# Cross-attention of a four-block kernel: the maximum over partitions by a turned row and a product of ones, the key bias as one product, other PSUM banks for the outputs, and an order of its own for each engine

## The reference, cut to what matters

```python
n = layernorm(x)                                            # per token, over 128 features
Sim = (n @ w1)[:, :, None] + (ctx @ w2)[:, None, :] + einsum('bid,bjd->bij', n * w3, ctx) + b_sim
A = softmax(Sim, axis=2)                                    # over the 77 context rows
hat = A @ ctx
Batt = softmax(max(Sim, axis=2), axis=1)                    # over the 512 tokens
hc = einsum('bi,bid->bd', Batt, n)                          # one vector for a batch element
feats = concat([n, hat, n * hat, n * hc[:, None, :]])
x = x + feats @ W_qv + b_qv
```

## Time and profile before

| | us |
|---|---|
| median of three runs | 1986.94 |
| the profiled execution | 1985.58 |
| its span in the trace | 1983.8 |
| first block, to the end of its last instruction | 108.74 |
| first instructions of the second block | 109.58 |
| mean granted TensorE clock over the span | 0.97 of full |

### The profile page before, as it was taken

The page is one execution under the profiler, slowest core; times in us unless marked ns, Lnnn a source line. Parts: engine busy times, 40 slices in busy tenths (PEclk is TensorE's granted clock), DMA queues, the critical chain, the costliest instruction groups (busy, mean ns, idle before and its releaser), DMA issues. The chain is left out here.

```text
span 1983.8 us, 78949 instructions
## 1 busy us (share of the span) xinstructions
PE 1823.7 (92%) x32837; PEld 1278.3 (64%) x32837; DVE 1430.1 (72%) x2605; ACT 1138.5 (57%) x2379; POOL 1435.6 (72%) x1838
## 2 busy tenths in 40 slices
PE   4769999999999999999999999999999999788948
PEld 3636666666666666666666666666666676566638
DVE  2268778778777788787878787877788778455546
ACT  1136666666566566666666566656666666335425
POOL 1168888879788888888888788978898888222334
PEclk9789999999999999999999999999999999889969
DMA  3022131111311113111113111121111101030012
GB/s 101 1 41 56 44 99 52 47 45 51 101 48 48 51 48 100 49 50 48 48 48 103 48 48 46 34 85 32 32 35 36 42 24 35 10 98 1 23 35 71
DMA packets 60837, 99.93 MB, mean 50 GB/s; under 512 B 15848, under 2 KB 35065, under 8 KB 58643
## 3 DMA queue, kind: packets, MB, share of 16 engines
q1 hardware_dynamic: 58978, 91.72, 16.0%
q0 software_dynamic: 1504, 3.17, 0.5%
HBM read 44.50 MB, written 21.45 MB: 33 GB/s over the span
## 5 line engine op out<-in xcount | busy, mean ns | idle before, releaser
L1273 PE MATMUL b_bank_proj<-layer_weights,b_stream_t 128*128 128x512 f32 x1152 | 591.6, 615 | 13.6 <-DVE b_plain_moved L1069 9.7
L1069 DVE TENSOR_TENSOR b_plain_moved<-b_bank_proj,b_rope 128x1024 f32<-128x1024 f32 x384 | 467.6, 1221 | 100.2 <-ACT b_squares L903 96.9
L812 POOL TENSOR_TENSOR b_rotated<-b_plain_moved 128x1024 f32<-128x1024 f32 x192 | 453.4, 2361 | 45.4 <-DVE b_plain_moved L1069 45.4
L827 POOL TENSOR_TENSOR b_rotated<-b_rotated,b_inv_norm 128x1024 f32<-128x1024 f32 x192 | 365.3, 1902 | 15.1
L903 ACT ACTIVATE b_squares<-b_bank_proj 128x512 f32<-128x512 f32 x384 | 229.2, 597 | 248.4 <-PE b_bank_proj L1273 243.4
L1273 PEld LDWEIGHTS b_bank_proj<-layer_weights,b_stream_t 128*128 128x128 f32 x1152 | 187.9, 191 | 117.1 <-issue 57.1
L1075 DVE TENSOR_REDUCE b_norm<-b_squares 128x16 f32<-128x1024 f32 x192 | 232.2, 1209 | 42.7 <-ACT b_squares L903 42.4
L1281 PEld LDWEIGHTS b_bank_shared<-const_tables,b_rotated 128*128 128x128 f32 x1536 | 180.6, 143 | 72.2 <-issue 67.4
L1281 PE MATMUL b_bank_shared<-const_tables,b_rotated 128*128 128x128 f32 x1536 | 211.9, 276 | 3.8 <-POOL b_rotated L827 1.7
L832 POOL TENSOR_TENSOR b_probs<-b_probs,b_inv_sum 128x512 f32<-128x512 f32 x192 | 200.3, 1047 | 14.0 <-DVE b_inv_sum L1090 13.8
L1347 PEld LDWEIGHTS b_bank_shared<-b_attended_t,layer_weights 128*128 128x128 f32 x1536 | 182.9, 192 | 25.6 <-issue 23.9
(11 more groups left out here) (346 smaller groups left out, 2889.7 us busy)
## 6 DMA issues: line engine op xcount, KB each, us to landing
b_v_shifted<-b_v SPq DMA_DIRECT2D x192, 192.0 KB, 2.5
sorted_rows<-sorted_rows SPq DMA_DIRECT2D x66, 258.0 KB, 3.2
layer_weights<-L_ffn_Wqkv SPq DMA_DIRECT2D x6, 1536.0 KB
b_v_shifted<-b_v SPq DMA_DIRECT2D x72, 128.0 KB
layer_weights<-L_ffn_Wo SPq DMA_DIRECT2D x6, 512.0 KB
c_sorted_in<-sorted_rows SPq DMA_DIRECT2D x23, 129.0 KB, 2.0
layer_weights<-L_ffn_w SPq DMA_DIRECT2D x8, 256.0 KB, 5.9
c_w<-L_ffn_w SPq DMA_DIRECT2D x8, 256.0 KB, 5.7
```

The lines of the kernel that those rows point to most:

```text
L812: nc.gpsimd.tensor_tensor(out=turned[:, k, :], in0=pm[:, k, 0, :], in1=pm[:, k, 1, :], op=ALU.add).then_inc(add_done, 1)
L827: nc.gpsimd.tensor_tensor(out=tk, in0=tk, in1=repeat_last(rn[:, k, :], DH), op=ALU.mult).then_inc(rope_done, 1)
L1069: nc.vector.tensor_tensor(to, src.to_broadcast(shape), tab.to_broadcast(shape), ALU.mult).then_inc(mul_done, 1)
L1273: nc.tensor.matmul(out, xs[:, b, t * P:(t + 1) * P], w, start=True, stop=True).then_inc(proj_full, 1)
```

## The change

- The maximum over partitions leaves GpSimd. TensorE turns the column of 128 maxima into a row (`turned_highest`), VectorE reduces that row to one negated value (`highest_row`), TensorE multiplies a row of 128 ones with it, which gives it on every partition (`wide_highest`), and VectorE copies it to SBUF (`highest_wide`). The negation at L330 is gone.
- The key bias of all four tiles is one product with 308 columns that opens the accumulation, instead of one with 77 columns for each tile.
- The sum of the token weights: ScalarE accumulates over the four tiles while it forms the weights, and one product with ones replaces four.
- `keys` moves from VectorE: the scaling of the keys to GpSimd, the key bias with b_sim to ScalarE.
- `hat` goes to `bk_k[b]` and no longer waits for `context_weights`; `out` goes to `bk_n[b]`.
- The lists of TensorE, ScalarE, VectorE and GpSimd are written out and differ in order.

```diff
@@ GpSimd
-                def highest(b):
-                    pool.wait_ge(max_own, b + 1)
-                    nc.gpsimd.partition_all_reduce(mxa[:, b:b + 1], mx[:, b:b + 1], P, bass.bass_isa.ReduceOp.max).then_inc(max_all, 1)
+                def keys(b):
+                    pool.wait_ge(w_in, 16 * NIN)
+                    pool.wait_ge(cT_done, b + 1)
+                    nc.gpsimd.tensor_scalar(gT[:, b, :], cT[:, b, :], w3[:, 2:3], w3[:, 0:1], ALU.mult, ALU.add).then_inc(gT_done, 1)
 ...
                 for b in range(B):
                     first(b)
+                    keys(b)
                 for b in range(B):
-                    highest(b)
                     bias(b)
@@ ScalarE
+                def key_bias(b):
+                    if b == 0:
+                        act.wait_ge(w_in, 16 * NIN)
+                    act.wait_ge(u_full, b + 1)
+                    nc.scalar.activation(urow[:, b, :], bk_k[b][0:1, P:P + CTX], ACT.Identity, bias=bsim[:, :]).then_inc(u_done, 1)
 ...
-                    nc.scalar.activation(bw[:, b, :], nm[:, b, :], ACT.Exp, bias=nmx[:, b:b + 1], scale=-1.0).then_inc(batt, 1)
+                    nc.scalar.activation(bw[:, b, :], nm[:, b, :], ACT.Exp, bias=nmx[:, b:b + 1], scale=-1.0,
+                                         accum_out=bsum[:, b:b + 1]).then_inc(batt, 1)
 ...
+                context(0..3) normed_t(0) key_bias(0..3) normed_t(1) exponent(0) normed_t(2) weights(0) exponent(1) normed_t(3)
+                probs_t(0) weights(1) exponent(2) hat_t(0) probs_t(1) weights(2) exponent(3) hat_t(1) probs_t(2) weights(3)
+                hat_t(2) probs_t(3) hat_t(3)
@@ VectorE
+                def highest_row(b):
+                    dve.wait_ge(turned_max, b + 1)
+                    nc.vector.tensor_reduce(mxa[:, b:b + 1], bk_k[b][0:1, 2 * P:3 * P], AX.X, ALU.max, negate=True).then_inc(max_row, 1)
+
+                def highest_wide(b):
+                    dve.wait_ge(max_wide, b + 1)
+                    nc.vector.tensor_copy(nmx[:, b:b + 1], bk_k[b][:, 3 * P:3 * P + 1]).then_inc(max_neg, 1)
 ...
-                    dve.wait_ge(max_all, b + 1)
-                    nc.vector.tensor_scalar(nmx[:, b:b + 1], mxa[:, b:b + 1], -1.0, None, ALU.mult).then_inc(max_neg, 1)
 ...
+                statistics(0) normalise(0) statistics(1) statistics(2) normalise(1) highest(0) statistics(3) normalise(2)
+                highest_row(0) normalise(3) highest_wide(0) highest(1) shares(0) highest_row(1) highest_wide(1) highest(2)
+                context_weights(0) shares(1) highest_row(2) product(0) highest(3) highest_wide(2) residual(0) highest_row(3)
+                context_weights(1) shares(2) stream(0) highest_wide(3) product(1) shares(3) context_weights(2) residual(1)
+                product(2) stream(1) context_weights(3) residual(2) product(3) stream(2) residual(3) stream(3)
@@ TensorE
-                    for t in range(TILES):
-                        out = bk_n[b][:, t * CTX:(t + 1) * CTX]
-                        nc.tensor.matmul(out, eT[:, b, t * P:(t + 1) * P], gT[:, b, :], start=True, stop=False)
-                        last = nc.tensor.matmul(out, ones[0:1, :], urow[:, b, :], start=False, stop=True)
+                    nc.tensor.matmul(split(bk_n[b][:, 0:TILES * CTX], CTX), ones[0:1, :], repeat_mid(urow[:, b, :], TILES),
+                                     start=True, stop=False, skip_group_check=True)
+                    for t in range(TILES):
+                        last = nc.tensor.matmul(bk_n[b][:, t * CTX:(t + 1) * CTX], eT[:, b, t * P:(t + 1) * P], gT[:, b, :],
+                                                start=False, stop=True, skip_group_check=True)
+
+                def turned_highest(b):
+                    pe.wait_ge(max_own, b + 1)
+                    nc.tensor.transpose(bk_k[b][0:1, 2 * P:3 * P], mx[:, b:b + 1], ident).then_inc(turned_max, 1)
+
+                def wide_highest(b):
+                    pe.wait_ge(max_row, b + 1)
+                    nc.tensor.matmul(bk_k[b][:, 3 * P:3 * P + 1], ones[0:1, :], mxa[:, b:b + 1], start=True, stop=True).then_inc(max_wide, 1)
@@ sums
-                    for t in range(TILES):
-                        last = nc.tensor.matmul(bk_n[b][:, 1:2], ones, bw[:, b, t:t + 1], start=(t == 0), stop=(t == TILES - 1))
-                    last.then_inc(b_full, 1)
+                    nc.tensor.matmul(bk_n[b][:, 1:2], ones, bsum[:, b:b + 1], start=True, stop=True).then_inc(b_full, 1)
@@ hat
-                    pe.wait_ge(hc_done, b + 1)
-                    nc.tensor.matmul(bk_n[b][:, :], cb[:, b, :], pT[:, b, :], start=True, stop=True).then_inc(h_full, 1)
+                    nc.tensor.matmul(bk_k[b][:, :], cb[:, b, :], pT[:, b, :], start=True, stop=True).then_inc(h_full, 1)
@@ TensorE's list
+                context(0..3) normed_t(0) key_bias(0..3) scores(0) normed_t(1) turned_highest(0) scores(1) wide_highest(0)
+                normed_t(2) normed_t(3) turned_highest(1) scores(2) probs_t(0) wide_highest(1) sums(0) turned_highest(2) hat(0)
+                scores(3) out(0) wide_highest(2) probs_t(1) turned_highest(3) sums(1) hat(1) wide_highest(3) probs_t(2) sums(2)
+                out(1) hat(2) probs_t(3) sums(3) out(2) hat(3) out(3)
```

150 lines of the change are left out of this document (95 added, 55 removed).

## The result

The changed kernel takes 1952.96 us, the median of four runs between 1947.93 and 1954.16; the kernel before, run beside it, 1986.45 (1985.29 to 1989.4). The ratio is 0.9822, with a 95% interval of 0.9809 to 0.9836: 33.5 us less. It ran twice more beside other kernels: 1951.62 us, ratio 0.9824 [0.9796, 0.9851], and 1956.5 us, ratio 0.9826 [0.9797, 0.9854].

What follows compares the result with a forecast made beforehand. Waits, chiefly GpSimd's 14.7 us all-reduce rounds, bound the first block. 11.5 + 60.6 + 0.4 + 1.3 + 4.6 = 78.4, less 7 for the clock, 71.4; 1985.58 - 37.3, plus 1.4: 1949.6 us, range 1941 to 1961.

Steps and rivals of the forecast that it cites:

- TensorE's work at the slower level: First block: four elements' TensorE work at 1.2 GHz, 60.6 us without the first `normed_t`; `scores` 3.7 us per element.
- Gaps: TensorE's waits in the first block: 0.4 us before `scores(1)` for ScalarE's copy, 1.3 us before `out(3)`.
- The clock: Full 2.4 GHz level near the end of each `out` block, used by following work: saves 7 us.
- Tail: Residual, statistics, root and stream behind the first block's last product: 4.6 us to its end.
- Rival 1: Slower level stays throughout the first block: end at 78.4 us, time 1956.6 us; chance 0.12.
- rival 2: Full level from the start of the first block: end near 55 us, time 1932 to 1933 us; chance 0.05.
- Rival 3: First block: the maximum's crossings between TensorE and VectorE wait in in-order lists, 8 us, time 1957.6 us; chance 0.14.
- The diagnosis: In the first block, GpSimd's four all-reduce rounds of 14.7 us move the whole pipeline with them.
- theory A: Expectation for run B: GpSimd's turns set the first block's pace; end near 95, time 1972 us or less.
- The rest alike within 3 us: From the second block's first records to the end, both kernels' spans were to be alike within 3 us.
- rival 4: Layers behind the first block fall to the slower clock more often: 48 us at 0.96, time 1997 us; chance 0.04.
- The side moves: First block: keys on GpSimd cost at most 0.1 us seen, key bias on ScalarE taken as nothing, 0.7 with table loads.

Runs made afterwards that it cites:

- B: Kernel before with only the maximum over partitions moved to TensorE and VectorE, old order kept: 1989.74 us, ratio 1.0011.
- D: Kernel before with GpSimd's four bias additions first and its four all-reduces behind them: 1991.12 us, ratio 1.0036.
- H: Changed kernel with 36 short bf16 products (32 columns) added at the head of TensorE's list: 1947.28 us, ratio 0.9785.
- G: Changed kernel with 24 bf16 products of 512 columns added while TensorE waits for its tables: 1952.89 us, ratio 0.9843.
- I: Changed kernel with the old products of `scores` and `sums` put back: 1967.86 us, ratio 0.9889.
- J: Changed kernel plus 36 short products, earlier loads of input, unit matrix and ones, and second block's small parameters loaded in the first block: 1945.73 us, ratio 0.9773.
- A: Changed kernel with GpSimd's all-reduce and the negation put back, each before its bias addition: 1990.83 us, ratio 1.0013.

## Why the prediction was right, and where it was not

**The sum of the block** came out near: end at 68.12 us for a forecast of 71.4. By its terms, from the rows above:
- *Start of `scores(0)`*: 10.81 for 11.5 us, 0.7 early; the weights landed sooner, and the key biases before it started at 9.69 for the 10.29 that I took as fixed.
- *TensorE's work at the slower level*: busy 47.7 us between 10.81 and 63.5 (the five windows), 13.7 of them at the full level, so 61.4 at the slower one, for 60.6. Inside it `scores` cost 1.32 + 4 x 0.46 = 3.2 us for 3.7: I took 0.64 a pair from a row where a K=128 pair alternates with a K=1 pair; four K=128 pairs in a row take 1.78 to 1.92 us, 0.46 each. The turned row and the ones product cost 0.35 and 0.51 for 0.25 and 0.43.
- *Gaps*: 4.85 us for 1.7. The two that I named are there, 0.47 before `scores(1)` for 0.4 and 1.91 before `out(3)` for 1.3; four more, of 0.52, 0.72, 0.77 and 0.46, all on VectorE, I did not see.
- *The clock*: this term was the worst sized. I took 7 us, of 8.9 "used as before" and at most some 12; it was 13.7. The rise after each block of `out` is used by the work behind it, and with the new order that work is there without the old pauses.
- *Tail*: 4.64 us for 4.6.

The sum of these is 71.4 - 0.7 + 0.8 + 3.1 - 6.7 = 67.9, with 0.2 of rounding left to 68.1. So two errors, the gaps and the clock, went against each other. Rival 1 (the slower level stays) and rival 2 (the full level from the start) are both refuted by the windows. The rule that rival 2 stood on, in the Trainium skill's "TensorE: Matmul & The Clock Gate", Part 1, that sustained matmul work releases the throttle, isn't borne out here: TensorE was busy 27.08 of 28.79 us, and its rows kept the slower level until the first block of `out` was nearly over. Rival 3, waits on VectorE's list, is there in these four gaps, 2.5 us together, not 8. Of the signs, the idle time (4.85 us, under 6), the end of the first `scores` (14.1 us, by 16) and the second block's start (69.0 us) came out; `scores` at 3.2 us did not reach the 3.5 to 4.

**The diagnosis** was half wrong, and the total hid it. "The whole pipeline moves with GpSimd's round" holds as a fact of the rows and not as their only cause: taking the rounds away alone gave nothing in time (B), and neither did taking six of the eight pauses away (D). TensorE's order was a second limit of the same length. The forecast survived because I walked the new lists and did not subtract 4 x 14.7 us from the old block. Had the change been only its first part, the same reading would have forecast some 14 us (theory A of B, an end near 95 for 108.74), for none.

**"The rest alike within 3 us"** failed: 1883.0 for 1874.2 us. The prediction gave a change of more than 4 us there as a sign of being wrong, and by that sign this part of it is. The total is near partly by luck: the block's end 3.3 us early, the rest 8.8 us longer, and a median that lies 1.2 us below the profiled execution where I had added 1.4, leave some 3 of the 3.4 us. About 5 us of the 8.8 are located: they are in the stretch to W1, and whether they are there depends on how many records TensorE has ahead (H, and by accident G and I). H and J, which put back exactly the 36 records that the change took away, are also faster as a whole; G and I are not, so the 5 us are shown for that stretch and not for the whole time. I had looked for a loss there in rival 4, by another mechanism and with another size. The other 4 us are open: the stretch from W1 to the last block took 1496.0, 1499.8 and 1506.0 us in three executions of the changed kernel, 1496.9 in the one of before, so it varies by more than what is to be explained.

**The side moves** cost nothing that reached TensorE, as forecast: ScalarE's four key bias operations take 1.02 us with no table load beside them, and the keys 0.42 us each on GpSimd. One cost was not foreseen:

```profile
17.82 4.14 DVE L332 TENSOR_SCALAR a_normed<-residual,a_mean_var,a_rstd 128x128 f32<-128x128 f32 x4 [0.28 <-POOL a_rstd L224]
```

The four normalisations of an element take 1.08 us elsewhere; here, beside GpSimd's three additions (18.17 to 21.88), 4.14. The Trainium skill states a rule that fits ("SBUF — State Buffer", SBUF: two separate sides): GpSimd and VectorE share a pair of ports, which one instruction holds to its end while the other engine's, if it is of a kind that needs the pair, waits. Three additions ran, and 3.06 us were lost; that the ports are the reason was not tested. `normed_t(3)` starts at 22.02 with 0.72 us of waiting for it, all that reached TensorE.

## What to carry to other kernels

A round that two engines share has one length, whoever sets it. Before a part of a change is credited with a gain, ask what the round would be with that part alone, by walking the other engines' lists without it; two limits of the same length each look like the cause, and neither gives anything alone. Where a gain is smaller than the stage shows, compare the stretches behind it by milestones such as the issues of loads: here they led to a pause of 2 us in a step that no line of the change touches, and with 36 products in idle time it was gone. Then check such a find against the whole time of more than one kernel: two of four agreed here.

## What the runs showed of the hardware

- GpSimd idles 5.5 to 6.1 us before an all-reduce that follows usual operations and 6.7 to 7.7 us before the first usual operation after it (kernel before, A and D), and nothing between all-reduces that follow each other. The Trainium skill ("GPSIMD Engine Reference", 2.1 Instruction dispatch) gives about 6 us without a visible instruction for the first call to a freshly loaded routine; the trace agrees in its 5.53 and adds that it is paid again at each turn, and that the way back costs 6.7 us and more. The same page (4. When to use GPSIMD) calls GpSimd the only option for a reduction over partitions; the rows show TensorE and VectorE do one in 0.42, 0.27, 0.58 and 0.14 us.
- TensorE pauses at fixed places of its instruction stream, 125.75 records apart in all 14 traces: mostly not seen, 0.2 to 3.1 us where seen, 36 to 44 us in all over the 1640 us behind the second block's start. What it waits for was not shown: the trace names no releaser.
- Short fp32 products, one-column products and turnings left TensorE at 1.2 GHz from 10.81 to 39.60 us, though it was busy 27.08 of these 28.79 us. In the first block of the kernel before and of the changed one the level rose only late in the twelve pairs of an `out`; in G it also rose in the 512-column bf16 products.
- At the slower level, K=128 products of 77 columns take 0.46 us a pair in a row and 0.64 each when they alternate with K=1 products of as many columns. So the columns are not the difference; what in the alternation costs it was not tested apart.
